# Attention and a two-expert FFN on one core: weight folds in the first steps, the common order for batches 1 and 2, and a spread table list

## What is computed

```python
# attention, batch-normalised projections, one head, causal
xa = x @ (W_attn + A @ B).T
xa = (xa - mean(xa)) * rsqrt(var(xa) + 1e-5) * gamma + beta     # mean, var over all tokens
q, k, v = split(xa, 3)
y = softmax(causal(q @ k.T / sqrt(128))) @ v
x = layernorm(x + y @ W_proj.T @ (W_proj + A2 @ B2).T)
# mixture of experts, 8 experts, hidden width 512, the two best per token
probs = softmax(ln(x) @ router_w.T + router_b)
gates = the two largest, normalised
h_e = gelu(ln_e(x) @ w1[e].T + b1[e]);  ys_e = h_e @ w2[e].T + b2[e]
x = layernorm(x + sum_e gates_e * ys_e)
```

## Time and profile before

| | |
|---|---|
| runs | 429.62, 430.28, 431.0 us |
| profiled execution, its time | 429.71 us |
| its span | 428.0 us |
| TensorE matmul busy | 403.6 us (94%) |
| VectorE, ScalarE, GpSimd busy | 284.7, 324.5, 321.0 us (67%, 76%, 75%) |
| mean granted TensorE clock | 0.988 |

### The profile page before, as it was taken

How to read it: one execution, slowest core, us unless ns; L and a number is a source line. 1 busy time by engine, 2 the same in 40 slices (tenths; PEclk the granted TensorE clock), 3 DMA queues, 4 the chain that set the end, 5 groups by cost and what they waited for, 6 DMA issues and landing times.

```text
span 428.0 us, 14581 instructions
## 1 busy us (share of the span) xinstructions
PE 403.6 (94%) x3454; PEld 386.2 (90%) x3458; DVE 284.7 (67%) x1676; ACT 324.5 (76%) x830; POOL 321.0 (75%) x605
## 2 busy tenths in 40 slices
PE   7988799999998999999999999999999999999980
PEld 6966787998887999999999999999999999999980
DVE  2446687999999777655556555446676666666662
ACT  1226688999888788777888887888888888888851
POOL 7000276888888888888888788748878888788885
PEclk9999999999999999999999999999999999999995
DMA  9999511111113432454544455642333334333211
GB/s 226 318 402 385 132 41 34 40 48 48 42 47 103 130 93 84 127 148 118 147 130 121 114 146 148 187 121 79 106 101 107 105 109 113 102 90 105 66 32 37
DMA packets 45490, 51.69 MB, mean 121 GB/s; under 512 B 6610, under 2 KB 37074, under 8 KB 45410
## 3 DMA queue, kind: packets, MB, share of 16 engines
q1 hardware_dynamic: 37312, 31.46, 27.4%
q0 software_dynamic: 7728, 18.51, 12.7%
q10 hardware_dynamic: 370, 0.80, 0.6%
HBM read 28.23 MB, written 21.72 MB: 117 GB/s over the span
## 4 chain that ended last, share of the span: by engine, by line
PE 53%; DVE 18%; issue 9%; POOL 9%; SPq 4%; DMA 4%; ACT 2%; POOLq 0%; DVEq 0%; ACTq 0%
PE bank L869 19%; PE bank L884 19%; POOL r_z L601 5%; POOL out L607 4%; PE bank L684 3%; DVE x_all L1284 3%; PE bank L859 2%; DVE st L1296 2%; PE bank L675 2%; DVE lg L1227 2%; DVE ix L1312 2%; PE bank L733 1%; DVE masked L1203 1%; DMA x_all<-x 1%; SPq L433 1%
## 5 line engine op out<-in xcount | busy, mean ns | idle before, releaser
L884 PE MATMUL bank<-w2T,xT 128*128 x1136 | 150.3, 275 | 0.7 <-DVE yt L1464 0.7
L869 PE MATMUL bank<-xT 128*128 128x128 f32 x1136 | 150.7, 276 | 0.0
L884 PEld LDWEIGHTS bank<-w2T,xT 128*128 128x128 f32 x1136 | 138.2, 192 | 0.9 <-issue 0.9
L869 PEld LDWEIGHTS bank<-xT 128*128 128x128 f32 x1136 | 138.0, 192 | 0.0
L921 ACT ACTIVATE xT<-w1T,zero_col 128x512 f32 x139 | 100.4, 722 | 40.7 <-issue 35.1
L1464 DVE TENSOR_TENSOR yt<-bank,b_bc 128x128 f32<-128x128 f32 x142 | 41.5, 292 | 89.0 <-PE bank L884 82.0
L607 POOL DMA_INDIRECT out<-xT,xg x71 | 75.9, 1069 | 16.9 <-issue 16.5
L594 POOL DMA_INDIRECT queue<-xT,xg x71 | 72.2, 1017 | 18.2 <-POOL idle L592 14.1
L1058 ACT ACTIVATE xT<-bank 128x512 f32<-128x512 f32 x142 | 82.1, 578 | 2.4 <-PE bank L869 2.4
L573 POOL DMA_INDIRECT queue<-x_all x64 | 62.2, 971 | 12.6 <-issue 7.9
L921 ACT ACTIVATE xT<-bank,one_col 128x128 f32<-128x128 f32 x142 | 52.1, 367 | 8.8 <-PE bank L859 3.4
(11 more groups left out here) (233 smaller groups left out, 729.2 us busy)
## 6 DMA issues: line engine op xcount, KB each, us to landing
xg<-queue SPq DMA_DIRECT2D x71, 129.5 KB, 2.1
xg<-queue SPq DMA_DIRECT2D x71, 67.5 KB, 2.2
x_all<-x SPq DMA_DIRECT2D x16, 256.0 KB, 6.1
xT<-x_t SPq DMA_DIRECT2D x8, 512.0 KB, 10.4
w1r<-w_t SPq DMA_DIRECT2D x8, 256.0 KB, 6.4
w2T<-w_t SPq DMA_DIRECT2D x8, 256.0 KB, 11.4
queue<-xT,xg POOLq DMA_INDIRECT x71, 2.9
out<-xT,xg POOLq DMA_INDIRECT x71, 2.4
```

Of the source, the lines that this page charges most:

```text
L869: last = mm(bank[2 + s][:, h * P:(h + 1) * P], w1c[:, (q - 1) % WR, h * P:(h + 1) * P], xgT[:, s, :], start=True, stop=True)
L884: last = mm(bank[4 + s][:, 0:P], hs[:, s, h, :], w2T[:, bass.ds(e, 1), h, :].rearrange("p a d -> p (a d)"), start=(h == 0), stop=(h == HC ...
```

## The change

The folds of experts 3 to 6 move into `first_steps`, TensorE and ScalarE, and that of expert 7 to the end of TensorE's step 3 with its copy in ScalarE's step 4. `EARLY`, `route` and `place` go: batches 0, 1 and 2 are routed, ranked and placed as all others are (batch b's one-hots in step b+3, its rank and place in step b+4). On ScalarE roots(0) stands later in `first_steps`. The list's parts stand behind the row maxima and behind the search for the best experts' indices instead of at the step's start and end, and their settle asks only for operations up to the list's previous part. The list's values stand 32 columns apart in `tab_w`, so that one product with the identity brings row starts and experts of both halves to partitions 0, 32, 64 and 96; `take_table` is one copy of all 128 partitions, and `value_load` reads from these four. `tab_w` is set to zero in the setup.

```diff
-        tab_p = sb("tab_p", [P, 2, 2, 2])
-        tab = sb("tab", [1, 2, NTILE], I32)
-        tab_row, tab_e = tab[:, 0, :], tab[:, 1, :]
+        tab_w = sb("tab_w", [P, 2, 2, 2, 32])
+        tab_p = tab_w[:, :, :, :, 0]
+        tab = sb("tab", [P, N1], I32)
+        def tab_at(kind, j):
+            row = 32 * (j // N1 * 2 + kind)
+            return tab[row:row + 1, j % N1:j % N1 + 1]
...
+            pg.did(pool.memset(tab_w[:], 0.0))
...
             def first_steps():                       # TensorE
+                later = iter(range(W1_FIRST, E))
                 pe.wait_ge(s_mt, 1)
                 make_z(0)
+                fold_w1(next(later))
                 scores(0, 0)
                 make_z(1)
+                fold_w1(next(later))
...
                 make_z(2)
+                fold_w1(next(later))
                 attend(0)
...
                 make_z(3)
+                fold_w1(next(later))
                 attend(1)
                 start_v(2)
                 make_v(2)
-                rank(0)
...
-                if has[4] and k - 4 > EARLY[-1]:
+                if has[4]:
                     rank(k - 4)
...
-                if k - 3 in EARLY:
-                    rank(k - 3)
...
-                if W1_FIRST <= k - FOLD_AT + W1_FIRST < E:
-                    fold_w1(k - FOLD_AT + W1_FIRST)
+                if k == PROLOGUE:
+                    fold_w1(E - 1)
...
                 pe.wait_ge(s_tabp, g + 1)
-                for c in range(2):
-                    for kind in range(2):
-                        at = (2 * c + kind) * P
-                        last = mm(bank[6][0:1, at:at + P], tab_p[:, g, c, kind:kind + 1], ident[:], start=True,
-                                  stop=True)
-                last.then_inc(s_tabt, 1)
+                mm(bank[6][:, 0:P], tab_w[:, g].rearrange("p c k n -> p (c k n)"), ident[:], start=True,
+                   stop=True).then_inc(s_tabt, 1)
...
             def first_steps():                       # ScalarE
                 copy_z(0)
+                copy_w1(next(later))
                 copy_z(1)
                 exponentials(0)
+                copy_w1(next(later))
                 copy_p(0)
                 copy_v(0)
                 copy_z(2)
                 exponentials(1)
+                copy_w1(next(later))
                 copy_v(1)
-                roots(0)
                 copy_p(1)
                 copy_z(3)
                 exponentials(2)
+                copy_w1(next(later))
+                roots(0)
                 copy_v(2)
                 copy_v(3)
...
-                if W1_FIRST <= k - 1 - FOLD_AT + W1_FIRST < E:
-                    copy_w1(k - 1 - FOLD_AT + W1_FIRST)
+                if k - 1 == PROLOGUE:
+                    copy_w1(E - 1)
                 if has[0]:
                     exponentials(k)
...
                 row_max(2)                           # VectorE
                 invert(1)
-                route(0)
-                place(0)
...
-                if known >= COUNT0:
-                    list_first_group(2 * (known - COUNT0))
...
                 if has[0]:
                     row_max(k)
+                if known >= COUNT0:
+                    list_first_group(2 * (known - COUNT0))
...
+                if known >= COUNT0:
+                    list_first_group(2 * (known - COUNT0) + 1)
                 if has[4]:
                     v.wait_ge(s_rk, b4 + 1)
...
-                if k - 3 in EARLY:
-                    place(k - 3)
-                if k - 2 in EARLY:
-                    route(k - 2)
-                if known >= COUNT0:
-                    list_first_group(2 * (known - COUNT0) + 1)
...
                 if n in range(3, 14):
-                    pg.settle()
+                    pg.settle(listed[0])
...
-                for c in range(2):
-                    first = c * N1 + g * NTILE0
-                    op(v.tensor_copy(tab[:, :, first:first + N_TILES[g]],
...
+                op(v.tensor_copy(tab[:, g * NTILE0:g * NTILE0 + N_TILES[g]], bank[6][:, 0:N_TILES[g]]))
```

More of the change, by code:

```diff
@@ L318, in build, with tab_row, tab_e @@
         picked = sb("picked", [P, 2, 2, 2, NPART])
-        tab_p = sb("tab_p", [P, 2, 2, 2])
-        tab = sb("tab", [1, 2, NTILE], I32)
-        tab_row, tab_e = tab[:, 0, :], tab[:, 1, :]
+        tab_w = sb("tab_w", [P, 2, 2, 2, 32])
[4 more added lines that the diff above has]
+            return tab[row:row + 1, j % N1:j % N1 + 1]
+        def tab_row(j):
+            return tab_at(0, j)
+        def tab_e(j):
+            return tab_at(1, j)
         ends_i = sb("ends_i", [1, 2 * E], I32)
@@ L329, in build @@
         s_rows, s_pad2 = [sem(n) for n in ("s_rows", "s_pad2")]
-        PROLOGUE, EARLY = 3, (1, 2)
-        FOLD_AT = 6
+        PROLOGUE = 3
         LIST_AT, LIST_STEPS, TAKE_AT = 8, 12, 22
@@ L432, in load_rows @@
                 wait(sp, s_yo[slot], j // XR * 16)
-                row = sp.value_load(tab_row[0:1, j:j + 1], min_val=0, max_val=DUMMY + (E - 1) * P)
+                row = sp.value_load(tab_row(j), min_val=0, max_val=DUMMY + (E - 1) * P)
                 if j < N1:
@@ L1028, in fetch_w1 @@
             def fetch_w1(k, q):
-                e = act.value_load(tab_e[0:1, bass.ds(k, 1)], min_val=0, max_val=E - 1)
+                e = act.value_load(tab_e(k), min_val=0, max_val=E - 1)
                 wait(act, s_h, k - WR + 1)
@@ L1228, in logits @@
                                           in1=r_bias[:], op0=ALU.mult, op1=ALU.add))
-            def route(b):
-                v.wait_ge(s_rr, b + 1)
-                for t in range(TPB):
-                    logits(b, t)
-                pg.settle()
-                for t in range(TPB):
-                    op(v.max(mx8[:, t, :], lg[:, t, :]))
-                pg.settle()
-                op(v.tensor_tensor(gd[:, of_batch(b)], mx8[:, :, 1], mx8[:, :, 0], ALU.subtract))
-                for t in range(TPB):
-                    op(v.max_index(ix8[:, t, :], mx8[:, t, :], lg[:, t, :]))
-                pg.settle()
-                v.tensor_tensor(one_hots(b), iota_e[:].unsqueeze(1).unsqueeze(1).to_broadcast([P, TPB, 2, E]),
-                                ix8[:, :, 0:2].unsqueeze(3).to_broadcast([P, TPB, 2, E]),
-                                ALU.is_equal).then_inc(s_oh, 1)
-            def place(b):
-                v.wait_ge(s_rk, b + 1)
-                op(v.tensor_tensor(ohr[:], one_hots(b), rkb, ALU.mult))
-                pg.settle()
-                with nc.allow_low_precision(reason="whole numbers below 2**24"):
-                    v.tensor_reduce(x_int[:, of_batch(b), POS1:POS2 + 1], ohr[:], AXX, ALU.add).then_inc(s_pos, 1)
             def first_steps():
@@ L1264, in first_steps @@
                 invert(1)
-                route(0)
-                place(0)
             def attend_step(k, q, use, known):
                 has = {d: 0 <= k - d < NB for d in (0, 1, 2, 3, 4)}
-                has[3] = has[3] and k - 3 > EARLY[-1]
-                has[4] = has[4] and k - 4 > EARLY[-1]
-                if known >= COUNT0:
-                    list_first_group(2 * (known - COUNT0))
                 b2, s2, b3, s3, b4 = k - 2, k % 2, k - 3, (k - 3) % 2, k - 4
@@ L1407, in list_first_group @@
                     finish_table(0)
+                listed[0] = pg.n
                 if n == 13:
@@ L1460, in add_bias @@
             def add_bias(j):
-                e = v.value_load(tab_e[0:1, j:j + 1], min_val=0, max_val=E - 1)
+                e = v.value_load(tab_e(j), min_val=0, max_val=E - 1)
                 v.wait_ge(s_yy, j + 1)
```

8 lines of the change are left out of this document (3 added, 5 removed).

## The result

The changed kernel takes 424.93 us, the median of 4 runs (424.56 to 426.97), against 430.43 of the kernel before on the same chip (4 runs, 429.62 to 431.0). The ratio is 0.9877, with a 95% interval of 0.9845 to 0.9908: faster, by 5.5 us between the medians and by 5.0 between the profiled executions (424.67 against 429.71). The direction was right, and so was the path in the changed kernel; the size was too small.

The account below looks back on a forecast made before the run. GpSimd's scatter queue, then SyncE, was taken to set tile 29 and the end: gate(0) about 2.0 us later, 5.3 us of waits gone, 3.3 net. 429.71 - 3.3 = 426.4, plus 0.57 gives 427.0; range 425.0 to 429.0.

Parts of the forecast that it names:

- The path: GpSimd's scatters and stores, then SyncE's loads and pads, set tile 29's start and the end; both 3.3 us earlier.
- Four folds and the last fold: First steps to step 4: four folds put 1.6 us on the path, the last fold 1.07 and its copy 0.58.
- Batches 1 and 2, and so gate(0): Steps 4 and 5: both 1.16 us one-hot stalls go, one ahead of gate(0), which moves about +2.0 us.
- What GpSimd gets back: First scatter to batch 29: 97.21 us becomes 91.9 unbroken, 5.3 us of waits gone; batch 29 3.3 us earlier.
- The Trainium skill's rule: GpSimd's scatters: a denser VectorE would stretch the queue by the rule; the prediction added nothing for it.
- SyncE and the pads: SyncE's 19.5 us stretch of loads and pads before tile 29 moves with GpSimd's store, unchanged in length.
- The list: Nine list steps 1.2 us shorter, the table's products 0.75 less, on TensorE's and VectorE's side; worth nothing at the end.
- TensorE's side: Steps 3 to 12 5.6 us earlier, some 7.5 with list and table; then 4.6 us waiting between tiles 25 and 29.
- Small parts: Setup memset of the spread list and table reads from four partitions: both taken as nothing.
- rival C: No change: four-row table reads cost SyncE 0.4 us in each of eight loads, or first steps cost double; chance 0.16.
- Rival D: Slower: five unhidden folds delay gate(0) by 7.4 us, end 2.1 later, 432.4; decisive from gate(0) at 55.2; chance 0.06.
- rival B: More comes through: gate(0) not late, 5.3 less, 425.0; or TensorE's whole 7.5 arrives, 422.8; together 0.16.

Follow-up runs that it names:

- e1: Changed kernel with three more memsets of 128 x 384 on GpSimd ahead of batch 12's scatters; 426.66 us, ratio to the kernel before 0.9902.
- e2: Changed kernel with six more unneeded products of 128 columns at the end of TensorE's step 12; 424.96 us, ratio to the kernel before 0.9879.
- e3: Changed kernel with expert 7's fold at the end of step 12 instead of 3, its copy in step 13; 423.64 us, ratio to the kernel before 0.9839.
- e9: Changed kernel with fold 7 in step 12 and the first pads behind the loads of tiles 17 to 24; 422.77 us, ratio to the kernel before 0.9821.
- e4: Changed kernel with SyncE's eight first pads behind the loads of tiles 17 to 24 instead of 21 to 28; 424.16 us, ratio 0.9841.
- e12: Changed kernel with late fold 7, early pads and GpSimd's per-batch memset cut from 128 x 384 to 128 x 64; 421.16 us, ratio 0.9801.
- e10: Kernel before with only the common order for batches 0, 1 and 2, folds and list as before; 427.08 us, ratio 0.993.
- e5: Kernel before with only the folds moved (four into the first steps, the fifth to step 3's end), on the slow chip; 446.34 us, ratio 0.9983.
- e11: Changed kernel with the list and the table as they were before; 425.32 us, ratio to the kernel before 0.9893.
- e6: Kernel before with only the common order for batches 0 to 2, on the slow chip; 445.07 us, ratio 0.9958.
- e7: Changed kernel with the list and table of before, on the slow chip; 445.96 us, ratio 0.9972.
- e8: Same kernel as e12 (late fold 7, early pads, shorter memset), on the slow chip; 463.07 us, ratio 1.0328.

## Why the prediction was right in kind and short in size

*The path (GpSimd, then SyncE, then TensorE).* Shown for the changed kernel. A delay on GpSimd comes through (e1: store +1.56, tile 29 +0.93), one on TensorE doesn't (e2: store +0.08, 1.35 us of idle still there at tile 29), the same fold at another place does (e3: store -1.49, tile 29 -1.19), and with both halves of the wait gone TensorE alone is in the chain (e9). The times go the same way, as differences of medians, each against the kernel before on its own chip: 5.5 us gained by the change, 3.3 with e1's delay, 5.0 with e2's, 6.4 in e3, 5.8 in e4, 7.5 in e9 and 8.8 in e12. The ratios put e1 at 4.2, e3 at 6.9 and e4 at 6.8. Their intervals are some 1.0 to 1.6 us to each side, so the single steps rest on the positions and only the order and the ends on the times. For the kernel before the path is less sure than I wrote: TensorE was ready at most 0.57 us before the rows there, in an execution whose last pad landed more slowly (3.64 us) than in any of the five others of this kind, and no experiment delays or relieves the kernel before itself. And e10 shows that with the new order alone the path is TensorE's. The two queues run close together, and the change had to move both.

*The sum that I warned of.* The prediction says that whoever adds up the slow places forecasts some 7 us. Its own numbers, five times 1.2, twice 1.4 and nine times 0.5, make 13.3; 7.5 is what it later worked out for TensorE's side, with the work that stays taken off.

*Four folds and the last fold.* Their price was right. Against e10, which has the new order without folds, step 3 starts 1.46 later (13.39 and 11.93 from make_z(0); forecast 1.57), step 4 2.54 later (forecast 2.64) and gate(0) 3.10 later (forecast 3.22).

*Batches 1 and 2, and so gate(0): the step that failed.* I took -1.16 for the order at gate(0), and it is -1.86 (e10). Two amounts are missing from the term. rank(0) leaves the first steps, and with it 0.41 of step 3's start (12.34 to 11.93); I wrote "a little for rank(0)" and put no number to it. And step 4 up to the gate is 1.44 shorter (4.68 to 3.24), 0.28 more than the recorded idle, probably since with the stall the rest of rank and what follows it on three engines is also moved. So gate(0) is at +1.24 instead of +2.06, the sum of the prediction's terms before it is rounded; of the 0.82 between them 0.70 are this term and 0.12 the folds'. The folds by themselves, without the new order, cost 1.65 at gate(0) (e5, read with the caution above): part of their time lies in the stall that the order removes, which is gone from step 4 in e5. With e10 this says that the parts can't be priced singly and added: -1.86 and +1.65 make -0.21, together they are +1.24.

*What GpSimd gets back.* 91.99 us from the first batch to batch 29 against 91.9 worked out from the batches without a wait. Right to 0.1. With gate(0) at its measured place the forecast for batch 29 would have been 143.1; it is at 143.22.

*The Trainium skill's rule.* SBUF — State Buffer, section "SBUF: two separate sides", has the descriptors of a DMA from GpSimd wait while VectorE runs a two-port copy. From 82 to 99 us VectorE is busy 17.00 of 17.00, and GpSimd's batches stay at 3.12 us. This trace does not show the rule at work, but it does not test it either: VectorE's rows in that stretch hold no copy, so a full VectorE, which is what the prediction argued with, was not the rule's condition.

*SyncE and the pads.* Priced at nothing, measured at -0.37, inside SyncE's own spread; and the last pad's landing, also priced at nothing, at -1.18. That landing is 3.64 us before and 1.78, 2.70, 2.06, 2.46 and 2.50 in e1, e2, e3, after and e11. No edit tells these apart, and of before there is one profile. Whether 3.64 was chance, or whether the denser start of the change has something to do with it, stays open. It is half of what the forecast lacks at tile 29, 5.66 - 3.3 = 2.4 us: GpSimd has 0.7 of it (gate(0)'s term above), SyncE 0.4, this landing 1.2, the load 0.1. Had it been 2.46 before as well, tile 29 there would have been earlier by at most the 0.57 by which TensorE was ready before the rows, and the change would still be worth 5.1 at tile 29 (an estimate from the table). So for the account of this one execution the landing matters, and for what the change is worth mostly that both queues moved, TensorE's by more.

*The list.* Nothing at the end that can be told apart, as forecast (e11). On TensorE's side the list and the first table product are worth 0.59 at the entry of the FFN, not 1.2 + 0.75. The table has a second product, at tile 20 in the FFN, which the prediction left out: 1.03 us before, 0.39 at 174.93 after.

```profile
181.11 1.03 PE L841 MATMUL bank<-ident,tab_p 128*1 128x128 f32 x8
```

The step from tile 20 to 21 takes 2.95 us before (2.95 to 2.96 in e10 and e11) and 2.20 after, so another 0.75 goes there.

*TensorE's side.* 7.45 us earlier at the FFN's first transpose, forecast 7.5, and the agreement is luck. Up to step 13 TensorE is 6.46 earlier (49.71 and 43.25 from make_z(0)), forecast 5.6; the list and the table then give 0.99, forecast 1.95. Two misses cancel. And of the 4.6 us of wait that I wanted between tiles 25 and 29, 1.19 are recorded as idle; by the starts of tiles 27 to 29 (2.42 and 2.96 us apart, where 1.90 is a step without a wait) it is 1.58. The missing 3.0 can be placed at tile 27, ahead of these waits. TensorE is only 6.68 earlier there (163.72 and 157.04), 0.8 less than forecast: it loses 1.42 up to tile 20, most of it near the half clock, and wins back 0.75 by the table's second product. The rows are 2.36 earlier than forecast (5.66 against 3.3). Together that is 3.2, less the 0.17 by which the wait of the kernel before was longer than its recorded idle. In this kernel the clock's loss lies ahead of a wait for rows, so as far as these positions show it costs the end nothing.

*Small parts.* The memset's price can't be seen: the start of make_z(0), behind it, spreads over 2.6 us by itself. The partitions of the table: nothing, as taken. SyncE's stretch is 16.79 to 17.46 us with reads from four partitions, 16.97 to 17.28 with one (before, e10, e11), and rival C's 0.4 us for each read would have made it over 3 us longer. Rival D's gate(0) of 55.2 was never near (50.97). Of rival B the first half came near: its 425.0 is the measured 424.93, but not by its reason, as gate(0) is late after all.

## What to carry to other kernels

Before several places are summed, find the queue that the end hears, and price each edit by the position of that queue's first instruction and by whether it runs unbroken behind it; here TensorE's 7.45 us at the entry of the FFN were worth 5.66 at tile 29. And look how far the second queue is behind: where it is 0.5 us, a change that moves only one of them soon meets the other (e10). An edit that removes work and a stall in front of the same gate is priced by walking the engines with both in place, with every small instruction that leaves the stretch in the sum: added singly, the two parts missed the truth by over 1 us. Where the queue is the bound, move work that has no due time behind its first release: fold 7 in step 12 instead of step 3, and the pads among earlier tiles, gave 2 us more with the same work.

## What the hardware did that I had not expected

**TensorE's clock.** At the entry of the FFN the granted clock fell from 1.00 to 0.50, the 1.2 GHz level, for 3.4 us in the executions of after, e2 and e10 and for 6.8 in that of e9, and stayed at 1.00 in those of before, e1, e3, e4, e11 and e12; e5, e6 and e7 on their own chip have such falls too, between 139 and 157 us. Ahead of it TensorE is only partly busy (1.23 us of 2.45 in the changed kernel, with idle of 0.47 and 0.75). But e3 has the same waits at the same places, 0.47 and 0.83 us, and there the eight products run at full clock:

```profile
130.49 0.50 PE L774 MATMUL bank<-vs,prT 128*128 128x136 f32 x2 [0.47 <-ACT prT L929]
...
132.28 0.30 PE L867 MATMUL bank<-ident,xT 128*128 128x128 f32 x1 [0.83 <-DVE xT L1446]
...
132.42 1.12 PE L877 MATMUL bank<-xT 128*128 128x128 f32 x8
```

So such waits stand ahead of the fall, and they alone don't decide it; what does, no run here shows. From the FFN's first transpose to tile 20 are 41.0 to 41.6 us in the six executions with the clock at 1.00 and 41.6 to 42.5 in the four where it fell, so it costs some 0.8 us between the means. Where TensorE is the bound, as in e9, that reaches the end.

**A slow chip.** On the chip of e5 to e8 the kernel before took 447.78 us. In e8's waits from 60 to 135 us, with engine, line and releaser, then us in total, times and longest, stand waits for "remote" which the changed kernel elsewhere doesn't have:

```profile
ACT prT L929 <- remote: 14.2, 5, 3.5
```

and its granted clock in the attention steps was 0.91, here with TensorE busy 17.09 of 20 us:

```profile
80.00:100.00 20.00, 17.09 (x128) 15.05 (x129) 13.44 (x109) 14.61 (x63) 9.85 (x18) 0.91 0.09 29
```

What held the engines there I can't say. Nor is it the chip alone: e5, e6 and e7 took 445 to 446 us on it, less than the kernel before, and only e8 463. The 0.7% that the new order gains elsewhere (e10) reads as 0.4% there (e6), the 1.1% of e11 as 0.3% (e7), and the 2.0% of e12 as a loss of 3.3% (e8).
